# The 25 features beside the 128 pair squares: all of them squares, in rows of 32 per head, applied in quarters of the array

## What is computed

```python
def second_taylor_expansion(x):
    x0 = ones(..., 1)
    x2 = einsum('...i,...j->...ij', x, x) * 0.5 ** 0.5
    return concatenate([x0, x, x2.reshape(..., d * d)])
...
q = second_taylor_expansion(q * dh ** -0.5)
k = second_taylor_expansion(k)
kv_state = einsum('bhnd,bhne->bhde', k, v)
den = einsum('bhnd,bhd->bhn', q, k.sum(axis=2))
out = einsum('bhnd,bhde->bhne', q, kv_state) / maximum(den, 1e-5)
x = layernorm(x + out @ w_out)
x = layernorm(x + ffn(x))
```

## Time and profile before

| what | value |
|---|---|
| median of 3 runs | 583.84 us |
| the profiled execution: its own time | 585.66 us |
| its span in the profile | 583.9 us |
| mean granted TensorE clock | 0.982 of full |
| TensorE busy | 554.3 us (95%) |
| VectorE busy | 479.5 us (82%) |
| ScalarE busy | 465.2 us (80%) |
| GpSimd busy | 145.9 us (25%) |

### The profile page before, as it was taken

One profiled execution on the slowest core, in us unless ns is written; L12 is line 12 of the kernel. 1 busy time (PEld: TensorE's weight loads), 2 busy tenths in 40 slices (PEclk: granted clock), 3 DMA queues, 4 the chain that ended last, 5 costly groups with the idle time before them and its releaser, 6 DMA issues.

```text
span 583.9 us, 11628 instructions
## 1 busy us (share of the span) xinstructions
PE 554.3 (95%) x3730; PEld 414.3 (71%) x3730; DVE 479.5 (82%) x1008; ACT 465.2 (80%) x954; POOL 145.9 (25%) x215
## 2 busy tenths in 40 slices
PE   3869999999999999999999999999999999999994
PEld 2436786768778686868868686877868687786772
DVE  3675878989798898979799897979989897978664
ACT  4837797887969798896979888797988879797773
POOL 3431232123133213213222221412322141210000
PEclk9987999999999999999999999999999999999997
DMA  8000000000000000000000000000000000000000
GB/s 285 4 21 1 18 1 2 19 20 18 20 18 18 0 18 18 18 18 18 18 0 18 18 18 18 18 18 5 13 18 18 18 18 18 1 19 1 19 2 36
DMA packets 7366, 12.34 MB, mean 21 GB/s; under 512 B 816, under 2 KB 1840, under 8 KB 7344
## 3 DMA queue, kind: packets, MB, share of 16 engines
q1 hardware_dynamic: 7056, 11.93, 6.2%
q10 hardware_dynamic: 288, 0.13, 0.1%
HBM read 7.86 MB, written 4.19 MB: 21 GB/s over the span
## 4 chain that ended last, share of the span: by engine, by line
PE 83%; issue 3%; DVE 2%; ACT 1%; POOL 0%; POOLq 0%; DVEq 0%
PE fps L408 25%; PE fps L409 25%; PE ring L348 5%; PE ring L331 5%; PE ring L376 5%; PE ring L384 4%; PE ring L308 4%; PE ring L392 2%; PE ring L315 2%; PE fps L448 1%; PE ring L298 1%; PE fps L400 1%; DVE h L878 1%; PE ring L334 1%; PE ring L366 1%
## 5 line engine op out<-in xcount | busy, mean ns | idle before, releaser
L408 PE MATMUL fps<-hid_hi,w_hi 128*128 128x512 f32 x576 | 226.6, 393 | 2.1 <-DVE hid_lo L892 1.4
L409 PE MATMUL fps<-hid_lo,w_hi 128*128 128x512 f32 x576 | 226.4, 393 | 0.0
L408 PEld LDWEIGHTS fps<-hid_hi,w_hi 128*128 128x128 f32 x576 | 108.2, 188 | 26.3 <-DVE hid_lo L892 3.7
L665 ACT ACTIVATE hid_hi<-fps,col 128x512 fp32r<-128x512 f32 x128 | 88.2, 689 | 45.4 <-PE fps L409 45.0
L409 PEld LDWEIGHTS fps<-hid_lo,w_hi 128*128 128x128 f32 x576 | 108.3, 188 | 22.5
L892 DVE TENSOR_TENSOR hid_lo<-fps,hid_hi 128x512 fp32r<-128x512 f32 x128 | 88.2, 689 | 26.3 <-ACT fps L666 23.4
L617 ACT ACTIVATE phiT<-ring 128x512 f32<-128x512 f32 x128 | 73.7, 598 | 15.9 <-PE ring L331 15.9
L666 ACT ACTIVATE fps<-fps,col 128x512 f32<-128x512 f32 x128 | 84.5, 660 | 0.0
L878 DVE SCALAR_TENSOR_TENSOR h<-fps,col,gate_zo 128x512 f32<-128x512 f32 x64 | 47.9, 748 | 35.9 <-ACT gate_zo L652 32.5
L247 DVE TENSOR_TENSOR phi_k<-phi_k 128x896 f32<-128x896 f32 x64 | 69.6, 1092 | 2.2 <-ACT v_one L589 1.7
L1032 POOL TENSOR_TENSOR k_mid<-phi_k,v_one 128x256 f32<-128x256 f32 x32 | 21.5, 673 | 160.4 <-ACT v_one L589 157.4
(11 more groups left out here) (102 smaller groups left out, 911.0 us busy)
## 6 DMA issues: line engine op xcount, KB each, us to landing
x_b<-in_x SPq DMA_DIRECT2D x16, 256.0 KB, 2.6
out<-gate_zo SPq DMA_DIRECT2D x16, 256.0 KB, 2.0
w_raw<-in_h SPq DMA_DIRECT2D x2, 1024.0 KB, 9.1
w_raw<-in_w SPq DMA_DIRECT2D x3, 256.0 KB, 4.1
sel_raw<-in_sel SPq DMA_DIRECT2D x1, 384.0 KB, 5.8
w_qkv_raw<-in_w_kv SPq DMA_DIRECT2D x1, 128.0 KB, 2.8
const<-in_consts ACTq DMA_DIRECT2D x1, 115.0 KB, 3.0
w_qkv_raw<-in_w_q SPq DMA_DIRECT2D x1, 64.0 KB, 3.5
```

The lines of the kernel that those rows point to most:

```text
L408: nc.tensor.matmul(fps[:, bank, :], w_hi[:, o:o + P], hi, start=start, stop=False)
L409: return nc.tensor.matmul(fps[:, bank, :], w_hi[:, o:o + P], lo, start=False, stop=stop)
L665: nc.scalar.activation(hid[1 - layer][0][:, m, :], fps[:, bank, :], ACT.Gelu, scale=scale)
```

## The change

All 25 remaining features of a head become squares: the 8 sums of pairs 8 apart, the constant, and the 16 values each with 1 added, (q_e + 1) squared. They take 32 rows for each head. So q goes to `restq` through a product with `sel`, one for each group of four heads (`rest0`, `rest1`), and through one square of 128 partitions each, with a column of zeros and ones added (`shift_c`). The copies of `q_linear` are gone. On the host the columns of `w_q` are put in another order, so that heads 0, 1, 4, 5 lie in `qT[0]` and heads 2, 3, 6, 7 in `qT[1]`.

On the keys' side, the constant and the squares of the single values are made to match: GpSimd's `k_small` has two small instructions more and one wait more (`k_half`). `spread_rest` is one instruction, `st_rest` and `w_rest` have 128 columns instead of 256, with one transpose. `apply_rest` makes four products of 64 rows and 64 columns, one for each quarter of the array; two of them (one for each half of the rows) go to the same 64 output partitions, in different banks.

In `RING`, `sq8` becomes `rest0`, `rest1` is new in bank 2 behind `sq4`, and `sq5` moves from bank 2 to bank 0.

```diff
 RING = (
...
-    ("sq0", FRONT, 3), ("sq1", FRONT, 0), ("sq8", FRONT, 2), ("sq2", FRONT, 1), ("sq3", FRONT, 3), ("sq4", FRONT, 0),
-    ("sq5", FRONT, 2), ("state", FRONT, 1), ("sq6", FRONT, 3), ("sq7", FRONT, 2))
+    ("sq0", FRONT, 3), ("sq1", FRONT, 0), ("rest0", FRONT, 2), ("sq2", FRONT, 1), ("sq3", FRONT, 3), ("sq4", FRONT, 0),
+    ("rest1", FRONT, 2), ("sq5", FRONT, 0), ("state", FRONT, 1), ("sq6", FRONT, 3), ("sq7", FRONT, 2))
...
+            def rest_of_q(t, g):
+
+                wait_q_lo(t, g)
+                bank_wait(RING, ring_free, t, f"rest{g}")
+                nc.tensor.matmul(ring[:, bank_of(RING, f"rest{g}"), :], sel[:, 4 * P:5 * P], qT[g][:, :],
+                                 start=True, stop=True).then_inc(ring_full, 1)
...
             def transpose_rest(t):
                 pe.wait_ge(st_rest_ready, t)
                 bank_wait(RING, ring_free, t, "restT")
-                for g in range(2):
-                    mm = nc.tensor.transpose(ring[:, bank_of(RING, "restT"), g * P:(g + 1) * P],
-                                             st_rest[:, g * P:(g + 1) * P], ident)
-                mm.then_inc(ring_full, 1)
+                nc.tensor.transpose(ring[:, bank_of(RING, "restT"), 0:P],
+                                    st_rest[:, :, :, :].rearrange("p g j f -> p (g j f)"), ident).then_inc(ring_full, 1)
...
-                for h in range(H):
-                    g, hh = h // 4, h % 4
-                    nc.tensor.matmul(ring[32 * hh:32 * hh + 32, bank_of(RING, f"acc{g}"), :], w_main[:, 32 * h:32 * h + 32], phiT[:, h, :],
-                                     start=True, stop=False)
-
-            def apply_rest(t):
-                pe.wait_ge(ring_free[bank_of(RING, "restT")], read(RING, t, "restT"))
                 for g in range(2):
                     for hh in range(4):
-                        h = 4 * g + hh
-                        mm = nc.tensor.matmul(ring[32 * hh:32 * hh + 32, bank_of(RING, f"acc{g}"), :], w_rest[:, 32 * h:32 * h + 32],
-                                              restq[g][:, :], start=False, stop=True)
+                        f = 4 * (hh // 2) + 2 * g + hh % 2
+                        if (g, hh) == (1, 3):
+
+                            pe.wait_ge(ring_free[bank_of(RING, "restT")], read(RING, t, "restT"))
+                        nc.tensor.matmul(ring[32 * hh:32 * hh + 32, bank_of(RING, f"acc{g}"), :],
+                                         w_main[:, g * P + 32 * hh:g * P + 32 * hh + 32], phiT[:, f, :],
+                                         start=True, stop=False)
+
+            def apply_rest(t):
+                for g in range(2):
+                    rows = slice(64 * g, 64 * g + 64)
+                    for q in range(2):
+                        heads = slice(64 * q, 64 * q + 64)
+                        mm = nc.tensor.matmul(ring[heads, bank_of(RING, f"acc{g}"), :], w_rest[rows, heads],
+                                              restq[q][rows, :], start=False, stop=True)
                     mm.then_inc(ring_full, 1)
...
-                    if f < H:
-                        op = nc.scalar.activation(phiT[:, f, :], ring[:, bank, :], ACT.Square)
-                    else:
-                        nc.scalar.activation(restq[0][64:P, :], ring[64:P, bank, :], ACT.Square, bias=one_c[64:P, :])
-                        op = nc.scalar.activation(restq[1][0:64, :], ring[0:64, bank, :], ACT.Square,
-                                                  bias=one_c[0:64, :])
-                    op.then_inc(ring_free[bank], 1)
+                    nc.scalar.activation(phiT[:, f, :], ring[:, bank, :], ACT.Square).then_inc(ring_free[bank], 1)
+
+            def square_rest(t, g):
+                bank = bank_of(RING, f"rest{g}")
+                act.wait_ge(ring_full, written(RING, t, f"rest{g}"))
+                nc.scalar.activation(restq[g][:, :], ring[:, bank, :], ACT.Square, bias=shift_c)\
+                    .then_inc(ring_free[bank], 1)
...
-            def q_linear(t):
-
-                bank = bank_of(RING, "qT")
-                nc.vector.tensor_copy(restq[0][0:64, :], ring[0:64, bank, :])
-                nc.vector.tensor_copy(restq[1][64:P, :], ring[64:P, bank, :]).then_inc(ring_free[bank], 1)
...
-                half_sum = v_one[:, j0:j0 + 2, :, SIG:SIG + 1].to_broadcast([P, 2, H, DH])
-                nc.gpsimd.tensor_tensor(k_mid[:, :, :, :], k, half_sum, ALU.subtract).then_inc(k_mid_ready, 1)
+                half_sum, ones = (v_one[:, j0:j0 + 2, :, n] for n in (SIG, DEN))
+                nc.gpsimd.tensor_tensor(k_half[:, :, :], half_sum, neg_half[:, 0:2].unsqueeze(2).to_broadcast([P, 2, H]),
+                                        ALU.subtract).then_inc(k_half_ready, 1)
+                nc.gpsimd.tensor_tensor(phi_k[:, j0:j0 + 2, :, ONE], ones, half_sum, ALU.subtract)
+                pool.wait_ge(k_half_ready, 2 * t + pair + 1)
...
```

More of the change, by code:

```diff
@@ L144, in build @@
         st = sb("st", [P, 2, FEAT])
-        st_rest = sb("st_rest", [P, 2 * P])
+        st_rest = sb("st_rest", [P, 2, 2, 32])
         w_main = sb("w_main", [P, 2 * P])
-        w_rest = sb("w_rest", [P, 2 * P])
+        w_rest = sb("w_rest", [P, P])
         wide = sb("wide", [P, 4 * N])
@@ L192, in build @@
         ring_free = [sem(f"ring_free{b}") for b in range(4)]
-        phi_k_ready, k_mid_ready, k_small_ready = sem("phi_k_ready"), sem("k_mid_ready"), sem("k_small_ready")
+        phi_k_ready, k_half_ready, k_mid_ready, k_small_ready = (
+            sem(n) for n in ("phi_k_ready", "k_half_ready", "k_mid_ready", "k_small_ready"))
         st_rest_ready = sem("st_rest_ready")
@@ L317, in project_q, with wait_q_lo @@
                 mm.then_inc(ring_full, 1)
[L319 to L336 removed]
+            def wait_q_lo(t, g):
+                if g == 0:
+                    pe.wait_ge(q_lo_ready, t + 1)
+                else:
+                    pe.wait_ge(ring_free[bank_of(RING, "qT")], read(RING, t, "qT"))
+            def sums_of_q(t, f):
+                g, l = f // 4, f % 4
+                if f == 0 and is_step(t, 0):
+                    pe.wait_ge(sel_ready, 1)
+                if l == 0:
+                    wait_q_lo(t, g)
+                bank_wait(RING, ring_free, t, f"sq{f}")
+                nc.tensor.matmul(ring[:, bank_of(RING, f"sq{f}"), :], sel[:, l * P:(l + 1) * P], qT[g][:, :],
+                                 start=True, stop=True).then_inc(ring_full, 1)
+            def rest_of_q(t, g):
+                wait_q_lo(t, g)
+                bank_wait(RING, ring_free, t, f"rest{g}")
+                nc.tensor.matmul(ring[:, bank_of(RING, f"rest{g}"), :], sel[:, 4 * P:5 * P], qT[g][:, :],
+                                 start=True, stop=True).then_inc(ring_full, 1)
             def state(t):
@@ L562, in second_step_sums @@
                 transpose_x1(1, 0)
-                for f in (0, 1, 8, 2, 3, 4, 5):
+                sums_of_q(1, 0)
+                sums_of_q(1, 1)
+                rest_of_q(1, 0)
+                for f in (2, 3, 4):
                     sums_of_q(1, f)
+                rest_of_q(1, 1)
+                sums_of_q(1, 5)
             peeled(steps_with(False), 0)
@@ L1071, in _ @@
             nc.gpsimd.memset(v_one[:, :, :, :], 1.0)
-            nc.gpsimd.memset(phi_k[:, :, :, ONE:ONE + 1], 1.0)
-            nc.gpsimd.memset(st_rest[:, :], 0.0).then_inc(consts_set, 1)
+            nc.gpsimd.memset(st_rest[:, :, :, :], 0.0).then_inc(consts_set, 1)
             pool.wait_ge(consts_loaded, 16)
@@ L1100 @@
     data["scales"] = _np.concatenate([c.reshape(-1, 128).T for c in columns], axis=1)
-    row = _np.arange(128)
-    head = row[:, None] // 32 == _np.arange(4)[None, :]
+    row, f = _np.arange(128)[:, None], _np.arange(128)[None, :]
+    rest = _np.arange(REST)[None, :]
+    scale = _np.where(rest == ONE - MAIN, 1.0, 0.5)
+    part = f % 32
+    is_one, is_lin = part == ONE - MAIN, (part >= LIN - MAIN) & (part < REST)
     data["consts"] = _np.concatenate([
-        _np.eye(128), _np.repeat(head, DH, axis=1), _np.repeat(head, 8, axis=1) * 0.5, _np.full((128, 4), -0.5),
-        _np.where(row < DH, 1.0, 0.5)[:, None], _np.isin(row, (32, 96))[:, None],
+        _np.eye(128), *((row // 32 % 2 == j) * scale for j in range(2)), _np.full((128, 4), -0.5),
+        _np.where(row < DH, 1.0, 0.5), (is_one | is_lin).T,
     ], axis=1).astype(_np.float32)
-    of_head, e = (row % 64 // DH)[:, None], (row % DH)[:, None]
-    f = _np.arange(128)[None, :]
+    of_head, e = row % 64 // DH, row % DH
     pairs = (e == f % DH) | (e == (f + f // DH) % DH)
     sums = [(of_head == hh) & pairs for hh in range(4)]
-    for at in (64, 0):
-        g = f - at
-        sums.append((g >= 0) & (g < 32) & (of_head == g // 8) & (e % 8 == g % 8))
+    eighth = (part < 8) & (e % 8 == part)
+    sums.append((of_head == f // 32) & (eighth | is_lin & (e == part - (LIN - MAIN))))
     data["sel"] = _np.concatenate(sums, axis=1).astype(_np.float32)
```

64 lines of the change are left out of this document (24 added, 40 removed).

## The result

The changed kernel takes 578.85 us (median of 6 runs, 577.25 to 580.26), the one before 583.50 (6 runs, 582.61 to 585.39). The ratio is 0.9918, with a 95% interval of 0.9896 to 0.9941: faster by 0.8%, a little more than the 0.5% that can be told from no change.

What follows compares the result with a forecast made beforehand. TensorE was busy all 33.71 us of a step, the vector side having 0.46 of slack; the new round summed to 33.71 again. So 583.84 + 13 x 0.0 - 1.1 = 582.7 us, range 574.5 to 588.8 (forecast's own 580.7 to 585.0).

Steps and rivals of the forecast that it cites:

- the forecast's 1.05: Price of `apply_rest`: two rounds, 0.87, plus 0.09 to enter and 0.09 to leave the form; 0.78 saved.
- TensorE's list: TensorE's own work in a middle step, forecast to fall from 33.71 by 0.78 and 0.11 to 32.82 us.
- the late wait at 225.01: TensorE's weight load behind VectorE, before the product at 225.37; used to price late waits at 0.05 plus 0.36.
- The wait at head 5: Head 5's moved sum waits for head 4's square; the state starts at 217.82 instead of 217.15, ScalarE idles 0.5.
- VectorE's 15.28: VectorE's gapless work from `x_lo` to the next step's third low tile of layer 2, taken as unchanged at 15.28 us.
- rival 3: GpSimd's longer lists slow VectorE's division, growing the round by 0.45: 588.6 us, chance 0.07.
- The round by the steps of the prediction: Chain of waits from layer 2's third low tile through TensorE, ScalarE and VectorE to the next step: 33.71 us.
- S: Moment when ScalarE's square of head 4 ends, forecast at 217.31, 7.68 after ScalarE's start at head 0.
- the vector side: The round through ScalarE and VectorE: 33.25 us before the change, so 0.46 of slack in a step.
- Start and end: Time outside the 13 middle rounds: first steps, third step and last attention step, together -1.1 us, bounds -2.5 and +0.5.
- Rival 1: ScalarE reaches head 4's square in time, so the round is 33.15: 575.4 us; chance 0.32 including what lies towards the forecast.
- the likeliest case: The whole kernel's time stays within 0.5% (2.9 us), no change that can be told; chance 0.46.

Runs made afterwards that it cites:

- e7: Kernel before, with two idle 16-element GpSimd instructions added ahead of each `k_mid`: 585.74 us, ratio 1.0032.
- e1: Changed kernel, with ScalarE squaring head 4's sum ahead of its copy of x1 instead of behind it: 572.17 us, ratio 0.9807.
- e4: Changed kernel, with two idle 16-element GpSimd instructions added ahead of each `k_mid`: 583.82 us, ratio 0.9994.
- e2: Changed kernel, with all four products of `apply_rest` put on rows 0 to 63 of the array: 590.04 us, ratio 1.0103.

## Why the prediction was right or wrong

**`apply_rest`: right in the mechanism, 0.08 short in the price.** From its own start to the next product it takes 1.02, two rounds of 0.43 and 0.15 to leave the form. But the 0.09 to enter it, which the forecast's 1.05 contains, lies ahead of that start: from `apply_main` to `apply_rest` are 1.85, where 1.74 is `apply_main`'s own work, so 0.11. (The wait for `w_rest` has moved into `apply_main` too; no run separates the two.) Both applications together take 2.87, where 1.74 + 1.05 = 2.79 was forecast, and 3.57 before: 0.70 saved instead of 0.78. The rule from the Trainium skill, TensorEngine Tiling (Array Packing), Key Properties, that a change of mode drains the engine, agrees with that.

**TensorE's list: nearly right, by terms that cancel.** Step less wait is 33.44 - 0.55 = 32.89, for a forecast of 32.82. Three things make the difference. The applications save 0.08 less; the sixteen products behind the keys' projection take 0.08 more (see e7); and the late wait at 225.01, which delays the product at 225.37 by 0.08 and which the forecast left inside the old list, is gone. (These are readings to a hundredth or two; no run takes the three apart.) In e1, where those products keep nearly their old pace, the list is 32.96 less 0.07 at the state's start and 0.08 behind the fourth low tile: 32.81.

**The wait at head 5: right in place, releaser and size.** The square of head 4 ends 7.60 behind ScalarE's start at head 0 (forecast 7.68), and the state starts 0.49 behind that (0.51). In all 0.55 late instead of 0.67; ScalarE's idle time is 0.36 instead of 0.5. The forecast let the rest squares cost the same on half the partitions as on all. They don't: the two halves start 0.70 apart, and behind the full one the next square starts 0.57 later (207.71, 208.28).

**VectorE's 15.28: here the prediction failed.** The low tile ends at 200.74 + 0.69 = 201.43, which is 234.87 in the next step, and `x_lo` starts at 219.83: 15.04. Of the missing 0.24 the division makes 0.21. I carried the duration of the row over, 0.90, although rival 3 said that it is 0.69 where the division starts ahead of GpSimd's instruction. GpSimd's timeline of before shows the other half of the overlap, and TensorE's the keys' projection:

```profile
197.81 0.66 POOL L1032 TENSOR_TENSOR k_mid<-phi_k,v_one 128x256 f32<-128x256 f32 x1 [9.10 <-ACT v_one L589]
```

```profile
229.67 0.37 PE L308 MATMUL ring<-w_qkv_hi,xnT_hi 128*128 128x264 f32 x1
```

The division starts 0.30 behind `k_mid`. From `x_lo` on VectorE's list is the same in both kernels: the division starts 6.47 and 6.48 behind `x_lo` (198.11 less 191.64, 192.86 less 186.38). But `k_mid` starts 6.17 behind it before and 5.96 after. Counted from `x_lo`, TensorE comes to the keys' projection 0.57 earlier behind the shorter `apply_rest` (4.34 before, 229.67 less 225.33; 3.77 after, 190.15 less 186.38), and the two new instructions give back only 0.36 of that. I had reckoned with these two alone, and so had the sign of the sum wrong. So the division now starts 0.52 behind `k_mid`, near its end.

The rows of all kernels follow one pattern: of two such instructions the later one ends about its own length behind the other's end, less some 0.15. The division ends 0.54 behind `k_mid`'s end in the kernel before (199.01, 198.47) and 0.56 in e4 (196.58, 196.02). In e7 `k_mid` is the later and ends 0.52 behind the division (198.67, 198.15). In the change `k_mid` ends at 192.98, 0.57 ahead of the undisturbed end of the division (193.55), so that the division pays nothing; the pair products behind it start after the division and end 0.34 behind it (193.89), 0.96 long instead of 0.49. The same step of the change shows both sides once more, at the second `k_small` (GpSimd's rows, then VectorE's features of k):

```profile
203.26 0.64 POOL L1046 TENSOR_TENSOR k_mid<-phi_k,k_half 128x256 f32<-128x256 f32 x1
203.85 1.34 POOL L1048 TENSOR_TENSOR phi_k<-phi_k 128x128 f32<-128x128 f32 x1
```

```profile
203.51 1.33 DVE L249 TENSOR_TENSOR phi_k<-phi_k 128x896 f32<-128x896 f32 x1
```

VectorE's instruction takes 1.33 where it takes 1.08 alone, and ends 0.94 behind `k_mid`'s end; the pair products end 0.35 behind VectorE's. It costs the step nothing there, since VectorE then stands idle for 0.85. With this pattern, and with the start of `k_mid` worked out, the forecast could have had the 0.69. The margin is thin: 0.57 where 0.54 is needed.

The round by the steps of the prediction, forecast and measured: to head 0's sum 2.01 and 2.07; to ScalarE 0.44 and 0.43; to S 7.68 and 7.60; to the state 0.51 and 0.49; to the copy 3.93 and 3.93; to the end of `x_hi` 3.83 and 3.85; 0.03 and 0.03; VectorE 15.28 and 15.04. The sums are 33.71 and 33.44. Without the 0.24 the vector side fell to a level that I had left unnamed: TensorE's own list and its wait at head 5, by the forecast's terms 32.82 + 0.67 = 33.49. That is what holds the step now. The third low tile isn't late any more (its product comes 0.23 behind the one ahead). The fourth tile's weight load waits 0.18, and the next product comes only 0.02 late for it, so the vector side lies just under the step: lengthen it by 0.34, as e4 does, and the step grows by as much. I had both terms and took only the larger round, without asking how far down the next one stands.

**Rival 3: the mechanism was right, its sign wrong here.** GpSimd's longer list touches VectorE through the division, and at a price of the forecast's order (up to 0.45; e4 shows 0.35 a step). But where the two meet decides who pays, and in the change VectorE gained 0.21. The Trainium skill, SBUF — State Buffer, Summary: rules for kernel authors, says that the later of two such instructions is held until the first has finished. In the runs the later one pays: GpSimd in e7 and the change, VectorE in e4 and before. And the ends given above nearly agree with a full hold: only some 0.15 of its own length is saved.

**Start and end: right in sum, not in place.** 13 steps by 0.263 (33.70 less 33.437) are 3.4; the medians differ by 4.65, so 1.2 is left for start and end, where 1.1 was forecast. But most of it lies in one step, the third: from the second spreading to the third are 31.80 us instead of 32.73 (50.14 to 81.94, 53.90 to 86.63), so 0.93 where the forecast had 0.3, and the kernels made from the change, apart from e2, have 31.78 to 31.80. That leaves 0.3 for steps 0 and 1 and the end, where 0.8 was forecast. At step 0 the transposes no longer stand idle for 1.03, and the application waits 0.39 for the copy of `w_rest`; at step 1 head 5's sum waits 0.90 for head 4's square, instead of 0.59 for the rest square, at granted clocks that differ.

**Rival 1** (575.4 us) was a matter of one place in a list: e1 moves one square by one place and comes to 572.17. That is below rival 1's own time, since e1 has the shorter division too (0.69): 33.15 less 0.24 is 32.91, and its steps are 32.96.

**The range and the chances: in part luck.** The time lies in the range because its lower end was put at rival 1. But what rival 1 asks for, ScalarE in time for head 4's square, didn't come; the gain came through the division, for which no term of the forecast stood. And the likeliest case, no change that can be told, had 0.46 and didn't come; the one that came, faster by over 0.5%, had 0.33.

## What to carry to other kernels

Where a change makes one round of waits shorter, work out the next two as well, and put the forecast between them: the step is the largest of TensorE's list with its waits and the vector side's round, and here they lay 0.2 apart. The duration of a VectorE instruction that overlaps a GpSimd instruction isn't a property of it but of who starts first, so in a forecast it is two values, with a condition, and any shift of either list by a few tenths can switch between them. And where a sum is moved behind a wait for another engine, look one or two places up in that engine's list: moving the awaited instruction ahead of one that nobody needs yet gave more here than the change itself.

## What the runs showed of the hardware

- GpSimd's instructions of 16 elements take 0.23 and start 0.18 apart. Two of them on an engine that is busy for 30% of the time cost the changed kernel 0.35 us a step (e4), though nothing reads what they write.
- A VectorE operation of 128x512 with two operands takes 0.69 alone, 0.90 when it starts 0.30 behind a GpSimd instruction of 128x256, and 1.03 at 0.17 behind. GpSimd's `k_mid` takes 0.66, and 1.16 when it starts 0.05 behind the VectorE operation. So either side can pay, and most when it starts just behind the other.
- Quarters of the array work at the same time on the same columns: four products of 64 by 64 take 1.02 to the start of what follows, and 1.86 when they share rows.
- TensorE's list can lengthen by 0.15 us in hundredths without a gap (e7), at a granted clock of 1.00. Why stays open.
